# Four layers of a graph network on one Trainium2 core: sums kept by rank in all layers, layer 4's two edge passes joined, and GpSimd making the one-hot columns of the last node stage

## The reference

```
x = ln(x + relu(segment_sum(x[src], dst) @ W0.T + b))                        # layer 1
h = batch_norm(cat(x[row], x[col], edge_attr_2) @ W1 + b1)                   # layer 2
x = ln(x + (segment_sum(relu(h) @ W2 + b2, row) / (count + 1) + x))
logits = sum(q[dst] * (k[src] + e)) / 4                                      # layer 3, 8 heads of 16
alpha  = segment softmax of logits over dst
conv   = segment_sum(alpha * (v[src] + e), dst) + x @ Wskip + bskip
h = ln(conv + x) ; x = ln(x + ln(ffn(h) + h))
score = exp(leaky_relu(src_score[src] + tgt_score[dst]) - max over all)      # layer 4, 4 heads of 32
x = ln(x + segment_sum(proj[src] * score / (segment_sum(score, dst)[dst] + 1e-16), dst) + bias)
```

## Time and profile before

| | before |
| --- | --- |
| median of 3 runs | 7105.09 us |
| lowest, highest | 7104.1, 7108.03 us |
| profiled execution | 7095.0 us, span 7093.3 us |
| mean granted clock of TensorE in it | 0.829 of full speed |
| busy: TensorE, VectorE, GpSimd, ScalarE | 71%, 67%, 65%, 34% of the span |

### The profile page before, as it was taken

How to read it: one execution, slowest core, us unless ns; L and a number is a source line. 1 busy time by engine, 2 the same in 40 slices (tenths; PEclk the granted TensorE clock), 3 DMA queues, 4 the chain that set the end, 5 groups by cost and what they waited for, 6 DMA issues and landing times. The chain is left out here.

```text
span 7093.3 us, 130837 instructions
## 1 busy us (share of the span) xinstructions
PE 5014.6 (71%) x26221; PEld 3720.7 (52%) x26221; DVE 4761.2 (67%) x15639; ACT 2418.4 (34%) x6817; POOL 4617.0 (65%) x4240
## 2 busy tenths in 40 slices
PE   6887997997565466667882587887777689988000
PEld 4665885555555422226772475444444489978000
DVE  5667995444555599986774566877777545567666
ACT  0113663111222244441110134766666611133333
POOL 5773777776888788886662003788888767600776
PEclk9998998998878788888896798988888855589555
DMA  4666996886555598886664344444444333344567
GB/s 151 208 205 197 272 264 192 261 260 164 71 70 71 95 276 263 263 239 189 203 206 91 98 148 122 104 99 101 100 104 99 90 94 99 97 140 160 145 153 146
DMA packets 1373314, 1118.61 MB, mean 158 GB/s; under 512 B 144636, under 2 KB 1169658, under 8 KB 1373020
## 3 DMA queue, kind: packets, MB, share of 16 engines
q1 hardware_dynamic: 1148316, 787.09, 37.7%
q0 software_dynamic: 175616, 238.28, 18.3%
q10 hardware_dynamic: 49200, 91.54, 3.9%
HBM read 590.08 MB, written 549.45 MB: 161 GB/s over the span
## 5 line engine op out<-in xcount | busy, mean ns | idle before, releaser
L445 POOL DMA_INDIRECT l_nodes_ag<-agg,l_nodes_at x784 | 787.5, 1005 | 1141.0 <-DVE l_nodes_at L439 590.3
L1484 POOL DMA_INDIRECT agg<-l_edges_b_rows,l_edges_b_at x392 | 610.5, 1558 | 130.1 <-issue 70.0
L2254 PE MATMUL l_nodes_f<-l_nodes_h_t_s,w_f 128*128 128x512 f32 x784 | 454.3, 711 | 209.2 <-ACT l_nodes_act_t L2197 209.0
L1654 PE MATMUL l_nodes_y<-w_qkvs,l_nodes_x_t 128*128 128x512 f32 x784 | 448.3, 725 | 190.6 <-DVE l_nodes_qkvs L1573 190.5
L514 POOL DMA_INDIRECT to_col<-l_nodes_col_s,l_nodes_rank_at x392 | 390.9, 997 | 226.0 <-ACT l_nodes_col_s L1174 121.1
L1734 POOL DMA_INDIRECT l_edges_a_kv<-kv_tab,l_edges_a_src_s x392 | 392.3, 1001 | 188.1 <-issue 107.5
L2160 POOL DMA_INDIRECT tgt_first<-l_nodes_ext,l_nodes_first_s x392 | 414.5, 1057 | 125.6 <-issue 113.8
L2370 POOL DMA_INDIRECT l_edges_a_proj<-proj_tab,l_edges_a_src_s x392 | 371.3, 947 | 174.6 <-issue 108.4
L227 ACT COPY l_edges_a_rows<-l_edges_a_sums 128x128 f32<-128x128 f32 (+1 forms) x784 | 160.1, 214 | 945.0 <-PE l_edges_a_sums L213 860.9
L1586 POOL DMA_INDIRECT q_first<-l_nodes_qkvs,l_nodes_first_s x392 | 403.2, 1029 | 108.8 <-issue 98.8
L1243 POOL DMA_INDIRECT l_edges_a_at_row<-to_row,l_edges_a_row_i x392 | 378.3, 965 | 131.0 <-issue 105.5
(11 more groups left out here) (324 smaller groups left out, 14737.2 us busy)
## 6 DMA issues: line engine op xcount, KB each, us to landing
agg<-zeros ACTq DMA_DIRECT2D x98, 516.0 KB
l_nodes_xg<-x SPq DMA_DIRECT2D x196, 256.0 KB
kv_tab<-l_nodes_qkvs SPq DMA_DIRECT2D x98, 512.0 KB
...
```

Of the source, the lines that this page charges most:

```text
L445: pool.indirect_dma_start(ag[k][:, j, :], None, table, bass.IndirectOffsetOnAxis(at[k][:, j:j + 1].bitcast(U32), 0),).then_inc(a_in[k][j], 16)
L1484: pool.indirect_dma_start(agg1[j // 2], bass.IndirectOffsetOnAxis(at[k][:, j:j + 1].bitcast(U32), 0), rows[k][:, j, :], None, compute_op=A ...
L1654: pe.matmul(y[j][:], x2_t[k][:, j, :], w_qkvs[:], start=True, stop=True).then_inc(y_done, 1)
L2254: pe.matmul(f[m % 2][:], w_f1[:, m * P:(m + 1) * P], h_t_s[k][:], start=True, stop=True).then_inc(f_done, 1)
```

## The change

`segment_steps` and `sum_fetcher` go; layers 3 and 4 use `compact_steps` and `window_steps` too. q and the target scores are scattered to tables by rank (`q_tab`, `tgt_tab`), `agg2` and `agg3` hold sums by rank. The zeroing of the two old tables in `edges_1a` goes, one of `agg2`, 49 DMAs of 1024 rows, is added to SyncE's work in `edges_1b`. The line of ranks is now two rows of bf16 halves, loaded in 2 KB, which TensorE multiplies with `radix` to 128 partitions (`spread_line`) and ScalarE copies from PSUM (`copy_line`), in every stage that loads a window. In `nodes_0` this takes a PSUM bank, and `col_p` has one buffer instead of two. `edges_2a`, `edges_2b`, `edges_3` become rotations with four buffers.

Layer 4's two edge passes are one, `edges_3`: per group TensorE spreads the targets, the maximum so far (`top`) goes over TensorE and VectorE to all partitions (`low`), `exp(score - top)` weighs the messages, and the carried sum is scaled by how far the maximum rose (`ease`). `nodes_3` loads the window and the 133 columns of `agg3` by one DMA a group; GpSimd compares (`mark_rest`, four instructions), TensorE multiplies (`spread_rows`, ten), ScalarE forms the scaled 1e-16 (`floor`, two Exp), and the square root of the norm moves from ScalarE to GpSimd. In the setup, `locate_sums` becomes `flag_nodes` and `rank_rows` makes the halves. Cut to its core, the steps of `edges_3` and `nodes_3` in the order of the functions, the diff is:

```diff
-            keys = [sb(f"keys{k}", [P, GE]) for k in range(RING)]
...
+            line = [sb(f"line{k}", [2, GE], BF16) for k in range(RING)]
+            keys = [sb(f"keys{k}", [P, GE]) for k in range(2)]
+            keys_p = ps("keys_p", [P, GE])
...
+                sp.dma_start(line[k][:], lines[bass.ds(n, 1)].squeeze(0)).then_inc(line_in[k], 16)
...
-                sp.dma_start(keys[k][:], lines[bass.ds(n, 1)].to_broadcast([P, GE])).then_inc(line_in[k], 16)
...
+            def spread_line(pe, i, k):
...
+                pe.wait_ge(line_in[k], i * 16 + 16)
+                if follows(i, k, 1):
+                    pe.wait_ge(line_copied, n)
+                pe.matmul(keys_p[:], radix[:], line[k][:], start=True, stop=True).then_inc(line_spread, 1)
...
+            def copy_line(act, i, k, made=(hot_made,)):
...
+                act.wait_ge(line_spread, n + 1)
...
+                    for s in made:
+                        act.wait_ge(s, n - 1)
+                act.copy(keys[k % 2][:], keys_p[:]).then_inc(line_copied, 1)
...
+            def mark_line(dve, i, k, used, some=range(G)):
...
+                dve.wait_ge(line_copied, n + 1)
...
-                for t in range(G):
-                    last = dve.tensor_scalar(hot[k % 2][t][:], keys[k][:, t * P:], own_rank[:, t:t + 1], None, ALU.is_equal)
+                for t in some:
+                    last = dve.tensor_scalar(hot[k % 2][t][:], keys[k % 2][:, t * P:], own_rank[:, t:t + 1], None, ALU.is_equal)
...
+            for j in range(G):
+                for t in range(j + 1):
+                    last = pe.matmul(out(j), hot[t][:, (j - t) * P:(j - t + 1) * P], ag[:, t, 0:width], start=(t == 0), stop=(t == j))
...
-                y, row_p, col_p = ([ps(f"{n}{m}", [P, G, D]) for m in range(2)] for n in ("y", "row_p", "col_p"))
+                y, row_p = ([ps(f"{n}{m}", [P, G, D]) for m in range(2)] for n in ("y", "row_p"))
+                col_p = ps("col_p", [P, G, D])
...
-                                pe.wait_ge(col_done, n - 1)
+                            if follows(i, k, 1):
+                                pe.wait_ge(col_done, n)
...
-                                last = pe.matmul(col_p[k % 2][:, j, :], x1_t[k][:, j, :], w1_ab[:, D:2 * D], start=True, stop=True)
+                                last = pe.matmul(col_p[:, j, :], x1_t[k][:, j, :], w1_ab[:, D:2 * D], start=True, stop=True)
...
-                        rotation(pe, groups, (2, spread), (8, turn_x1), (3, project), (9, project_x1))
+                        rotation(pe, groups, (0, lambda i, k: spread_line(pe, i, k)), (2, spread), (8, turn_x1), (3, project), (9, project_x1))
...
-                            act.copy(col_s[k][:], col_p[k % 2][:]).then_inc(col_done, 1)
+                            act.copy(col_s[k][:], col_p[:]).then_inc(col_done, 1)
...
-                        rotation(act, groups, (5, lambda i, k: root(act, i, k)), (2, copy_a), (8, copy_x1), (7, apply), (10, lambda i, k: stage_rank(act, i, k)), (10, col))
+                        rotation(act, groups, (0, lambda i, k: copy_line(act, i, k)), (5, lambda i, k: root(act, i, k)), (2, copy_a), (8, copy_x1), (7, apply), (10, lambda i, k: stage_rank(act, act.copy, i, k)), (10, col))
...
-                        pipeline(dve, pairs, (2, add_e), (0, stage), (1, lambda i, k: compare(dve, i, k)), (2, score), (2, flatten))
...
+                        rotation(dve, groups, (0, stage), (1, lambda i, k: mark_line(dve, i, k, q_spread)), (2, add_e), (2, score),
+                                 (3, flatten))
...
-                        pipeline(pe, pairs, (0, lambda i, k: turn_keys(pe, i, k)), (1, edge), (1, spread_q), (3, turn_logits))
+                        rotation(pe, groups, (0, lambda i, k: spread_line(pe, i, k)), (1, edge), (1, spread_q), (4, turn_logits))
...
+                mark, mark_carry, total, empty, store, settle, summed, evacuated = compact_steps(space, agg3, D + H3, ease)
...
+                            dve.tensor_tensor(both[k % 2][:], proj[k][:, :, D:D + H3], tgt_p[:, k % 2], ALU.add).then_inc(added, 1)
...
+                            dve.tensor_reduce(line_top[k % 2][:], top_p[:], AX.X, ALU.max).then_inc(line_topped, 1)
...
+                            dve.tensor_tensor(top[k % 2][:], line_top[k % 2][:], was[:], ALU.max).then_inc(topped, 1)
...
+                            dve.tensor_scalar(low[k][:], low_p[:], -1.0, None, ALU.mult).then_inc(lowered, 1)
...
+                        rotation(dve, groups, (0, stage), (2, score), (1, lambda i, k: mark_line(dve, i, k, tgt_spread)), (2, raise_top),
+                                 (2, lambda i, k: mark(dve, i, k, (3, 2))), (2, lower), (2, lambda i, k: mark(dve, i, k, (1, 0))),
+                                 (2, weigh), (2, carry))
...
...
+                        rotation(pe, groups, (2, turn_top), (0, lambda i, k: spread_line(pe, i, k)), (1, spread_tgt), (2, spread_top),
+                                 (3, total_messages))
...
+                            act.activation(msg[k % 2][:, :, D:D + H3], lifted[k % 2][:], ACT.Exp, bias=low[k][:]).then_inc(risen, 1)
...
+                            act.activation(ease[k][:], was[:], ACT.Exp, bias=low[k][:], scale=-1.0).then_inc(eased, 1)
...
-                ag, stage_rows, fetch, arrived = sum_fetcher(space, agg3, D + H3)
...
+                ag, hot, load_window, spread_line, copy_line, mark_line, window_in, hot_made, keys, line_copied = window_steps(
+                    space, agg3, width, node_base, node_line)
...
+                            pe.wait_ge(pool_made, n + 1)
+                            if follows(i, k, 2):
...
+                                pe.wait_ge(scaled, n - 1)
+                            spread_rows(pe, lambda j: sums[k % 2][j // half_g][:, j % half_g, :], hot[k % 2], ag[k], width).then_inc(spread, 1)
...
-                        rotation(dve, groups, (4, lambda i, k: balance(dve, i, k)), (2, mix))
+                        rotation(dve, groups, (6, lambda i, k: balance(dve, i, k)), (3, mix))
...
-                        rotation(pool, groups, (0, lambda i, k: fetch(pool, i, k)))
+                        def mark_rest(i, k):
...
+                            for t in range(G):
+                                last = pool.tensor_scalar(hot[k % 2][t][:], keys[k % 2][:, t * P:], own_rank[:, t:t + 1], None, ALU.is_equal)
+                            last.then_inc(pool_made, 1)
+                        rotation(pool, groups, (1, mark_rest), (5, lambda i, k: root(pool, i, k)))
...
+                                last = act.activation(least[k][:, some, :], sums[k % 2][m][:, :, D + H3:width], ACT.Exp, bias=floor_log[:])
+                            last.then_inc(floored, 1)
...
-                        rotation(act, groups, (0, stage), (3, lambda i, k: root(act, i, k)), (5, apply))
+                        rotation(act, groups, (0, lambda i, k: copy_line(act, i, k, (pool_made,))), (2, floor), (7, apply))
```

829 lines of the change are left out of this document (380 added, 449 removed).

## The result

The changed kernel takes 7465.01 us (median of 4, 7458.74 to 7470.55) against 7106.56 us: ratio 1.0503, 95% interval 1.0485 to 1.0521. The profiled execution has a span of 7457.0 us, 363.7 more than before.

What follows compares the result with a forecast made beforehand. Each stage has its own limit: TensorE in nodes_0, GpSimd's gathers in nodes_3 and nearly in edges_2a. Terms 294 + 184 - 160 - 48 - 12 + 4 = +262 on 7105 gave 7367 us, range 7090 to 7560.

Steps and rivals of the forecast that it cites:

- nodes_0: Stage nodes_0: one col_p buffer closes a loop through TensorE and ScalarE, 8.41 us a group; +294 us, bounds +226 to +342.
- second rival: In nodes_0 the loop does not close; only the line's 22 us is added, kernel 7095 us; chance 0.08.
- sum of 7.70: In nodes_0, the loop's pieces through both engines at full clock, 7.70 us an iteration against 5.28 before.
- the ends: In nodes_0, time outside the 98 iterations: 38 us, from 50 before less the turn-over that the longer iteration hides.
- nodes_3: Stage nodes_3: 392 gathers go, a loop through TensorE, ScalarE and VectorE remains, 6.85 us a group; +184, bounds +61 to +306.
- the cover: In nodes_3, GpSimd's compares (1.38 to 3.2 us) and root (about 1) lie beside the loop; 4.2 a group, under 5.59.
- price I had for GpSimd beside VectorE: In nodes_3, GpSimd computing beside VectorE could add 0.28 us a group, 28 us; a bound and no term.
- Layer 4 joined: Layer 4's two edge passes, 893 us with the gap, become one of 733 at clock 0.85; -160, bounds -267 to +340.
- third rival: The joined pass of layer 4 stays at the lower clock level, 1233 us; kernel 7867 us; chance 0.06.
- first rival: TensorE stays at the upper clock level in nodes_0, nodes_3 and layer 4; change -36, kernel 7069 us; chance 0.11.
- The rest: Other stages: edges_2a -48 (to 530 us), setup -12, edges_1b +4; edges_2b, edges_1a, nodes_1 and nodes_2 at 0.
- likeliest case: Whole kernel: the forecast of 7367 us, own range 7190 to 7510 from the terms' bounds as independent errors; chance 0.70.

## Why the prediction was right, point by point

**nodes_0**, +294 predicted, +339 measured. The mechanism, its place and its order are as written: the wait for `col_done`, behind `copy_x1` and `apply`. Undone in two ways, by the order (609 from start to start) and by the bank (614), it vanishes, and the second rival (the loop does not close) is refuted. The line's way over TensorE alone costs the 32 to 37 us that are left over 577. For this I had 22, at 0.22 a group: the rows show 0.50, of which 0.31 is the line and 0.10 the spread behind it (2.26 for 2.16).

Three sizes were off. The sum of 7.70 was 8.06 when the clock was up, by the same pieces: line 0.31 for 0.22, spread 2.26 for 2.16, the eight products to the next line 1.98 for 1.79; the hops were as I had them. Then the clock: I took 0.87, which the stage's row shows to the digit, but that mean counts the pause, which had 1.00. TensorE's part of the loop took 6.14 us in the iteration at 1003.50 (9.04 less the 2.90 from the turn's end at 1007.04 to 1009.94) and 5.15 at full clock (8.06 less 2.91 in the kernel with the pause filled), a ratio of 0.84: about 1.0 us a group went to the clock, and I had 0.71. And the ends: 98 iterations of 9.04 are 886 of the 896 us, so 10 remain for the 38 I had. This last error goes against the other two; without it the term would have missed by more than 45.

**nodes_3**, +184 and +189. The loop of products, `floor`, `apply` and multiplication is as written, and it opened when `apply` went first. That the number is right within 5 us is partly luck. The text put TensorE at under half of the time and took the middle between two levels for want of a row; TensorE was busy 64% of the stage and its products took 3.95 us, where the middle has 3.75. The rest of the loop took 2.91 for 3.09. On average an iteration is 7.09 us, 0.24 over the forecast, and of the 22 us for ends there is hardly any: the two errors cancel. The step that failed without harm is the cover: GpSimd's compares "cost between 1.38 us and 3.2", and took 4.76 (1568, 1245, 1351 and 596 ns for 512, 384, 256 and 128 columns), with the root's share 5.5 a group (538 us over 98). The text had 4.2 and GpSimd idle for a third of the time; it was idle for 23%. At full clock, where the loop would be 5.4 (6.86 with products of 2.5), they would have been level with it. With the loop opened they counted, and two of them on VectorE were worth more than the loop: 697, 627, 460.

The price I had for GpSimd beside VectorE, 0.28 us a group, was a mean of two things. In `nodes_1` of before, VectorE's L1560 took 0.69 us where GpSimd did something else or nothing, and over 2.1 the 19 times of 98 that it met GpSimd's addition of two tiles:

```profile
2809.26 0.69 DVE L1560 SCALAR_TENSOR_TENSOR l_nodes_u<-l_nodes_xg,l_nodes_u 128x512 f32<-128x512 f32 x1
...
2815.38 2.12 DVE L1560 SCALAR_TENSOR_TENSOR l_nodes_u<-l_nodes_xg,l_nodes_u 128x512 f32<-128x512 f32 x1
```

```profile
2815.65 1.30 POOL L1596 TENSOR_TENSOR l_nodes_x2b_s<-l_nodes_x2s,b 128x512 f32<-128x512 f32 x1
```

Beside the compares VectorE lost next to nothing: the multiplication L2380 took 419 ns, 420 with none on GpSimd. The rule of the Trainium skill, "GPSIMD Engine Reference", Key points, which names VectorE instructions of two SBUF inputs, had excused L2380, and the trace agrees. But the addition L2386, of two SBUF inputs, was spared as well: 700 ns beside the compares, 692 without. So what the rule names shows in `nodes_1` and not here. That it depends on what GpSimd does meanwhile is argued from these rows, not shown, since L1560 and L2386 are different operations.

**Layer 4 joined**, -160 and -76. This is the term that was mis-sized most. TensorE is never idle, as predicted, so the pass is product time only: 6.60 us at full clock for my 6.2 (line 0.31, targets 2.33 for 2.16, the steps of the maximum 0.5 for 0.3), and a clock of 0.80 for my 0.85. The estimate by time of its two sources, 0.81, which I had worked out and moved away from, had the right number, but not for its reason: it gives the targets' products 0.50 and the sums 0.98. In the trace it is mostly the sums that are slow: in the iteration at 6282 they had 0.50, behind targets' products at 0.94, and with the wide products their mean fell from 357 to 294 ns. It is the targets' products that bring it about all the same: made 64 columns wide, they leave the stage at 0.96 and 679 us. Why narrow products cost the ones behind them the clock is not shown. The third rival, 0.50 throughout, did not come about.

**The clock**: the first rival, 0.98 in all three loops, fell in each (0.87, 0.80, 0.70). The rule of the Trainium skill, "TensorE: Matmul & The Clock Gate", section "HAM oscillation — how this bites in real kernels", that waits between bursts of products bring the slow level back, agrees for `nodes_0`, where filling the wait brought 0.98, though the page's example has longer waits than these 2 us. It does not cover the joined pass, which had no waits and 0.80, and the prediction was wrong to lean its third rival on it.

**The rest**: `edges_2a` came to 509 for the 530 forecast. Gathers and issue are 491, and 20 remain of the 80.5 us of waits; the 30 for ends had no room in the stage before either, whose gathers, issue and waits (392.3, 107.5 and 80.5) fill its 578 us. The other 7 us of the row lie behind `edges_2a` and were not looked into. Small terms I had at nothing, `nodes_1` +10, `edges_2b` +9, `nodes_2` -13, cancel; what makes them was not looked into. The errors (45, 5, 84, -28, -6, -4, and 6 for the three small ones) make the 102 us between +262 and +364: the two big misses, in `nodes_0` and layer 4, go the same way, and what cancels is small. The median, 7465, lies inside the range and inside the likeliest case's own.
